# Two attention layers of a fused transformer kernel: the access patterns of two families of loads are rewritten

## The reference

```python
scores = q @ k^T * hd**-0.5 + rel_bias_table[bucket(j - i)]      # per head
out    = softmax(scores) @ v
```

```python
attn = q @ k^T
attn = attn + take_along_axis(q @ rpe_k_table, clip(j - i))      # query side
attn = attn + swap(take_along_axis(k*scale @ rpe_q_table, ...))  # key side
attn = softmax(attn)
out  = attn @ v + segment_sum(attn, clip(j - i)) @ rpe_v_table   # value side
```

## Time and profile before

| | us |
|---|---|
| median of three runs | 2232.39 (2231.03 to 2233.9) |
| the profiled execution's own time | 2231.06 |
| span of the profile | 2229.3 |
| DVE busy in the span | 1655.6 (74%) |
| ACT busy | 1064.4 (48%) |
| POOL busy | 839.8 (38%) |

### The profile page before, as it was taken

How to read it: one execution, slowest core, us unless ns; L and a number is a source line. 1 busy time by engine, 2 the same in 40 slices (tenths; PEclk the granted TensorE clock), 3 DMA queues, 4 the chain that set the end, 5 groups by cost and what they waited for, 6 DMA issues and landing times. The chain is left out here.

```text
span 2229.3 us, 46311 instructions
## 1 busy us (share of the span) xinstructions
PE 1787.1 (80%) x16408; PEld 1312.2 (59%) x16408; DVE 1655.6 (74%) x3948; ACT 1064.4 (48%) x2023; POOL 839.8 (38%) x632
## 2 busy tenths in 40 slices
PE   6999974888888975499999458888787669997656
PEld 3777752555555653378888235555454458886434
DVE  5999996776666756789999827999899662224674
ACT  4888853554554531145555315566555323332532
POOL 3000007755555501135444444444445119901111
PEclk8999997999999997699999757899898769998877
DMA  4111103000000000100000383544454150000000
GB/s 119 51 58 46 48 14 88 21 18 18 18 18 18 18 1 5 13 24 13 24 24 12 80 221 120 156 149 150 144 158 140 50 217 20 19 0 7 1 1 22
DMA packets 130615, 129.43 MB, mean 58 GB/s; under 512 B 76565, under 2 KB 107131, under 8 KB 129682
## 3 DMA queue, kind: packets, MB, share of 16 engines
q1 hardware_dynamic: 129522, 126.78, 19.1%
q10 hardware_dynamic: 928, 0.47, 0.1%
HBM read 78.59 MB, written 40.81 MB: 54 GB/s over the span
## 5 line engine op out<-in xcount | busy, mean ns | idle before, releaser
L2845 ACT ACTIVATE l2a_pr<-l2a_ps_s,l2a_nm 128x512 f32<-128x512 f32 x256 | 173.8, 685 | 142.4 <-DVE l2a_nm L2768 137.8
L529 ACT ACTIVATE l0a_pr<-l0a_sm,l0a_nm 128x512 f32<-128x512 f32 x256 | 185.0, 723 | 47.8 <-DVE l0a_nm L398 46.6
L398 DVE CUSTOM_DVE_ANT_0 l0a_sm<-l0a_ps_s,l0a_tb 128x512 f32<-128x512 f32 x256 | 174.8, 684 | 25.1 <-PE l0a_ps_s L613 18.5
L2775 DVE STREAM_TRANSPOSE l2a_tt<-l2a_pr 128x1024 f32<-128x1024 f32 x128 | 157.9, 1234 | 3.3 <-ACT l2a_pr L2845 3.3
L2768 DVE TENSOR_REDUCE l2a_nm<-l2a_ps_s 128x2 f32<-128x1024 f32 x128 | 156.7, 1224 | 4.4
L621 PE MATMUL l0a_ps_p<-top_c_ident,l0a_pr 128*128 128x128 f32 x1024 | 155.5, 274 | 0.0
L1703 POOL TENSOR_TENSOR l1f_h<-l1f_lm,l1f_sg 128x512 f32<-128x512 f32 x72 | 93.0, 1291 | 152.0 <-DVE l1f_lm L1769 75.9
L621 PEld LDWEIGHTS l0a_ps_p<-top_c_ident,l0a_pr 128*128 128x128 f32 x1024 | 128.7, 141 | 22.0 <-issue 0.9
L2102 ACT ACTIVATE l2f_h<-l2f_ps_h 128x512 f32<-128x512 f32 x128 | 76.4, 598 | 131.7 <-PE l2f_ps_h L1615 125.5
L1831 ACT ACTIVATE l1f_csb<-l1f_ps_c,l1f_b3e 128x512 f32<-128x512 f32 x128 | 88.1, 688 | 103.1 <-PE l1f_ps_c L1615 95.0
L2069 DVE SCALAR_TENSOR_TENSOR l2f_acc<-l2f_ps_y,l2f_comb,l2f_acc 128x128 f32<-128x128 f32 x112 | 31.5, 344 | 133.1 <-PE l2f_ps_y L2143 133.1
(11 more groups left out here) (535 smaller groups left out, 5122.3 us busy)
## 6 DMA issues: line engine op xcount, KB each, us to landing
l_qband<-l2a_staged SPq DMA_DIRECT2D x16, 768.0 KB, 15.8
l2a_qb<-l_qband SPq DMA_DIRECT2D x16, 768.0 KB
l2a_sb<-l_pband SPq DMA_DIRECT2D x32, 384.0 KB
l0a_tb<-l_bias SPq DMA_DIRECT2D x16, 448.0 KB
l2a_ks<-l_k SPq DMA_DIRECT2D x16, 384.0 KB
l_pband<-l2a_pr SPq DMA_DIRECT2D x32, 192.0 KB, 7.6
l_pband<-l2a_pr SPq DMA_DIRECT2D x32, 144.0 KB, 2.5
l2f_upw<-in_L_ffn_up_weights SPq DMA_DIRECT2D x9, 512.0 KB, 11.3
```

Source lines behind the costliest of these rows:

```text
L398: v.tensor_tensor_reduce(sm[j % 4][:, :], ps_s[j % 2][:, :], tb[slot][:, off:off + N][:, ::-1], -1.0, 3e38, ALU.add, ALU.min, nm[:, j % 4: ...
L529: a.activation(pr[j % 4][:, :], sm[j % 4][:, :], ACT.Exp, bias=nm[:, j % 4:j % 4 + 1], scale=-1.0).then_inc(m["p_ready"], 1)
L2775: v.transpose(tt[n % 2][:, u * NB:(u + 2) * NB, :].rearrange("p (u k) i -> p u (k i)", u=2), pr[g // 2 % PR_RING][:, 2 * (g % 2):2 * (g % ...
L2845: a.activation(pr[slot][:, 2 * (g % 2) + u, :], ps_s[g % 2][:, u, :], ACT.Exp, bias=nm[:, g % 2, u:u + 1], accum_out=rs[:, n % 2, 2 * (g % ...
```

## The change

The skewed loads of `q_load` and `s_load` become four transfers each, one for each batch: 32 rows of destination partitions from a source of two dimensions (32 rows, one row's elements). Each of the four adds 16 to the semaphore, so all thresholds on `qband_read` and `s_read` are multiplied by B = 4. In `load_parts` the number of transfers stays, but the two outer dimensions of the source change places: the 8 rows of a head outermost, the blocks inside. The rows of `qs` and `ks` thereby come in another order, the same for both, so the sum over the rows is the same.

```diff
 def load_parts(...):
     for first, count, q_part in PART_RUNS:
-        src = bass.AP(parts.tensor, parts.offset + off, [[0 if is_q else size, count], [parts.shape[2], HD], [1, parts.shape[2]]])
+        src = bass.AP(parts.tensor, parts.offset + off, [[parts.shape[2], HD], [0 if is_q else size, count], [1, parts.shape[2]]])
         queue.dma_start(dst[first * HD:(first + count) * HD], src).then_inc(sem, 16)
...
-def skewed(band, offset, step, width):
+def skewed(band, b, offset, step, width):
     pitch = width + GRP
-    return bass.AP(band.tensor, band.offset + offset, [[GRP * pitch, B], [pitch + step, GRP], [1, width]])
+    return bass.AP(band.tensor, band.offset + b * GRP * pitch + offset, [[pitch + step, GRP], [1, width]])
...
 def q_store(h):
-        sp.wait_ge(qband_read[before % 2], 16 * (before // 2 + 1))
+        sp.wait_ge(qband_read[before % 2], 16 * B * (before // 2 + 1))
...
 def q_load(h):
-    src = skewed(qband[h % QBAND_RING], GRP - 1, -1, ROW)
-    sp.dma_start(qb[h % 2][:, :, :].rearrange("p a n -> p (a n)"), src).then_inc(qband_read[h % 2], 16)
+    for b in range(B):
+        sp.dma_start(qb[h % 2][b * GRP:(b + 1) * GRP, :, :].rearrange("p a n -> p (a n)"),
+                     skewed(qband[h % QBAND_RING], b, GRP - 1, -1, ROW)).then_inc(qband_read[h % 2], 16)
...
 def p_store(o):
-        sp.wait_ge(s_read[before % 2], 16 * (before // 2 + 1))
+        sp.wait_ge(s_read[before % 2], 16 * B * (before // 2 + 1))
...
 def s_load(n):
-    sp.dma_start(sb[n % 2][:, :, :].rearrange("p a n -> p (a n)"), skewed(pband[n % PBAND_RING], 1, 1, HROW)).then_inc(s_read[n % 2], 16)
+    for b in range(B):
+        sp.dma_start(sb[n % 2][b * GRP:(b + 1) * GRP, :, :].rearrange("p a n -> p (a n)"),
+                     skewed(pband[n % PBAND_RING], b, 1, 1, HROW)).then_inc(s_read[n % 2], 16)
...
 # POOL
 def combine(h):
-    g.wait_ge(qband_read[h % 2], 16 * (h // 2 + 1))
+    g.wait_ge(qband_read[h % 2], 16 * B * (h // 2 + 1))
 def cut(n):
-    g.wait_ge(s_read[n % 2], 16 * (n // 2 + 1))
+    g.wait_ge(s_read[n % 2], 16 * B * (n // 2 + 1))
```

## The result

| | before | after |
|---|---|---|
| median, us | 2233.14 (2231.03 to 2235.13, 4 runs) | 2183.02 (2182.77 to 2185.29, 4 runs) |
| the profiled execution, us | 2231.06 | 2185.29 |
| span of the profile, us | 2229.3 | 2183.5 |

The ratio is 0.9778, with a 95% interval of 0.9761 to 0.9795: 50.1 us less, where 37 were forecast.

What follows compares the result with a forecast made beforehand. DVE bounds the third layer's loop, idling partly behind skewed loads carried by about 4 engines. Gains of 23.2 (loop), 9.0 (its start), 0.9 (its end) and 4.0 (first layer) sum to 37.1 us: 2195 us against the median, range 2184 to 2214.

Steps and rivals of the forecast that it cites:

- the width: Skewed and operand loads: outermost dimension sets the engines, 4 before and 16 after for skewed loads, 8 for load_parts pieces.
- the 15.2 us of band waits: Third layer's loop: DVE's band transpose waits for POOL's mask, 15.2 us; all were to go.
- the 2.6 us for ACT: Third layer's loop: DVE's transpose waits for ACT, late behind a store in full queues; all 2.6 us were to go.
- the start and the first layer: Start of the third layer's loop gains 9.0 us (bounds 4 and 9.5), the first layer's start 4.0 (2 and 4.5).
- SP: SP's queue: nine more issues a head, 5.4 us of its time, cost nothing while SP has that much free.
- the 13.5 us behind PE's scores: Third layer's loop, DVE's bias addition: 5.4 us of these waits go with band waits, 8 stay; bounds 0 and 13.5.
- (a): Rival, third layer's loop: half of the loop's gain turns into DVE waits on PE, 2207 us; chance 0.18.
- the end: End of third layer's loop: last sb load 2.2 us sooner, PE works until 1767.8; gain 0.9 us, bounds 0 and 1.5.
- (b): Rival, skewed loads: 32-row pieces are written at half rate, so start and tail lose about 2 us; 2199 us, chance 0.10.
- (c): Rival, skewed loads: pieces get no more engines than the whole load, last piece ends 1.8 us later; 2263 us, chance 0.05.
- (d): Rival, third layer's loop: SP becomes the bound if issues cost over 1.8 us; at 2 us each 2255 us, chance 0.03.

Runs made afterwards that it cites:

- the two-piece kernel: Against the changed kernel, each skewed load cut into two transfers of two batches each (outermost source dimension 2) instead of four of one; 2454.8 us, ratio 1.1023.
- operands at i = 6: Against the changed kernel, the next head's score operand loads issued at step i = 6 of the third layer's loop instead of i = 3; 2226.4 us, ratio 0.9984.
- the other execution of the old third layer: Only load_parts changed against the kernel before, the third layer left as it was; 2224.1 us, ratio 0.9981.
- eight pieces: Against the changed kernel, each skewed load cut into eight pieces of 16 rows instead of four of 32; 2189.5 us, ratio 0.9807.

## Why the prediction was wrong in size and right in kind

**Right: the width.** Four engines before, more after: shares of 0.23 and 0.24 became 0.62 and 0.37. That is 10 and 6 engines on average and not the 16 and 8 that the forecast named; neither stretch tells how many one piece had, since the pieces start one after the other. The rule that the forecast took from the Trainium skill ("DMA: Bandwidth & Descriptors", the part on how many engines a transfer gets) gives 2 engines for the two-piece kernel. The trace agrees: a share of 0.13 (2.1 engines) where little but skewed rows moved.

**Right: the 15.2 us of band waits and the 2.6 us for ACT** are both 0.0 after. The wait that takes their place is the one named, POOL for the key side's band, 9.5 us after the issue (10 was forecast).

**Right: the start and the first layer.** 8.9 us for 9.0 and 3.9 us (4.5 in the run with that part alone) for 4.0. PE's first scores came 15.8 us after the issue of `q_load(0)`, forecast 15.0 (1326.3 after 1311.26). DVE's first step then still waited, for POOL's `combine(0)`, which the forecast had not put last.

**Right: SP.** Three more issues for each load are hidden. Each costs 0.43 to 0.87 us in a group of four (1.7 to 3.5 us a group).

**Wrong: "Of the 13.5 us behind PE's scores ... 5.4 us go with them. The other 8 us I let stay, as PE alone may cause them where its clock is low".** This is the step that failed: a term that was sized too large. Only 3.3 us stayed (2.9 to 4.3 in the other five kernels whose `q_load` is in pieces and whose operands are not late), so 10.2 went.

The other half of the step, 5.4 us for eight waits that follow band waits, came out right, with some luck, since it rested on one sighting: there are nine such waits, 5.3 us, and they went with the band waits. What was mis-sized is the remainder, 8.2 us in ten waits, of which 4.9 went. The forecast took PE's low clock as a reason for them to stay. In rival (a) it said itself that fewer stops should raise the clock, but never put that into the sum. The runs show what such waits hang on: they stand behind stops of PE, whatever PE stood for. Behind a stop for `ks` alone DVE lost 0.61 us in each of 14 heads (operands at i = 6), behind a late band alone 0.68 us (`s_load` in pieces), both at a clock of 0.50. With the loads early the long stops are gone and the clock of the loop rises from 0.86 to 0.92. All eight waits that are left stand 3.1 to 3.7 us behind one of PE's shorter stops for DVE's band (1.2 to 2.6 us).

Part of the term was chance. Of the 8.2 us, 4.4 lie in the one stretch from 1380 to 1394 us that the other execution of the old third layer doesn't have; there only 1.7 us stood apart from the band waits. Why PE stayed at half clock for so long in that stretch is open. The forecast read one execution and called its remainder lasting. How the rest divides between stops for `ks` and stops for the band is not settled either, since in most heads both come together.

That is 4.8 of the loop's 7.5 us. Of the rest, 0.3 us are small gaps (5.5 before, 5.2 after). The other 2.4 us are in DVE's work as the profile counts it, 355.2 against 352.5 us (0.3 of this 2.7 is where the two stretches were cut). The groups shorten by 0.9 us only (the two shared with POOL's operands, 42.1 to 41.6 and 28.5 to 28.1); the records of neighbouring instructions overlap by about 0.1 us when nothing lies between them (the transpose before 1757.23 ends at 1757.32), so each of the some 21 waits that went (29 to 8) also gives back one such overlap. This last is read from the records and was not tested.

**Wrong: the end, 0.9 forecast, 3.2 measured.** The load came to POOL 3.5 us after its first issue, 6.6 before, so 3.1 us sooner instead of 2.2. And the floor that the forecast set, PE working until 1767.8, held only at the clock of before: 0.54 from 1758 to 1768 us; in the stretch of after that answers to it,

```profile
1717.00:1727.00 10.00, 8.68 (x121) 5.74 (x121) 4.80 (x12) 1.12 (x3) 1.40 (x2) 0.78 0.22 59
```

it is 0.78. It is the same error as in the loop: PE's time was taken as fixed, though its clock is one of the things that the change moves.

**The rest of the miss is chance.** The terms add up to 46.7; the medians are 50.1 apart because the profiled execution of before was 2.1 us under its median and that of after 2.3 above. Measured again on another chip, the change gave 0.9798 (0.9776 to 0.9821), 45 us of 2231, which is near the terms' 46.7.

**The rivals.** (a), PE takes the place of the loads, 2207: refuted, since the opposite happened (0.86 to 0.92). The step that spoke against it was the missing term. (b), 32-row pieces at half rate, 2199: not seen in the time. There is a trace of it in the engines' time. Per byte it is the share over the rate, 0.61/155 against 0.46/143, 22% more, and 34% more with 16-row pieces (0.67/156); not twice. That is for all bytes. In the stretch with the last `sb` load alone it is 0.62/177 against 0.23/89, 36% more. (c), pieces stay narrow, 2263: refuted by the shares; the two-piece kernel shows what still narrower ones cost. (d), SP as the bound, 2255: refuted by eight pieces.

## What to carry to other kernels

Read the outermost dimension of both sides of every transfer before its bytes. If it is 4, about four engines carry it (a share of 0.23 here), and other transfers and the issuing engine can be held up with it; cutting it where this brings a long dimension outermost was worth more here than its issues cost. A stop of PE has a price beyond the stop itself, also in a loop bound by another engine: look at the clock behind it and at who waits for PE there. And when a change takes long stops away, the low clock of before is no longer a floor; put its recovery into the sum. Before a remainder of waits is carried over as lasting, list them one by one, and if possible in a second execution: here more than half of it was one spell.

## What of the hardware was not expected

- A stop of 4.4 us of PE at each head costs DVE 3.2 us, in a loop where PE has some 20% of its time free: about 2.5 us of direct waiting, and 0.6 us in a second wait 3.4 us later, at a clock of 0.50 that had been 1.00 before the stop. Two kernels that differ in the place of three issues (i = 3 or 6) are 40 us apart.
- Transfers on four engines don't only take long themselves: with the `s_load` family alone in pieces the stops for `ks` fell from 34.8 to 5.6 us, though `ks` itself was loaded as before. SP no longer stood in the issue of these loads (83.2 us before, 17.8 then).
- Halving the outermost dimension from 4 to 2 costs far more than widening it from 4 to 32 gives: +228 us against -50. Once the loads no longer fit into the head, every engine waits for them.
- The time from issue to landing of a store that wasn't changed (`q_store`) fell from 15.8 to 5.8 us (medians). With `q_load` alone in pieces it was 5.9, with `s_load` alone 16.2. That its rows had stood behind those of `q_load`, which is issued just ahead of it, is the likely reason; no run moved one of the two to show it.
